# Two-layer recurrent kernel on one core: head of the next sequence one expert later on VectorE, last query product ahead of the second scores

## The reference, cut to what matters

```python
x = x + s * g
xn = _layernorm(x, axis=-1)
s = _L1_attn_ref(xn, ...)
g = _silu(_L1_ffn_ref(xn, ...))
x = x + s * g
```

## Time and profile before

| | |
|---|---|
| Median of 3 runs | 2175.03 us (2170.23 to 2177.49) |
| Profiled execution, its own time | 2173.18 us |
| Its span in the profile | 2171.3 us |
| Mean granted clock of TensorE | 0.971 of full speed |
| DVE | 1736.1 us busy, 80% |
| ACT | 978.4 us busy, 45% |
| POOL | 840.8 us busy, 39% |
| DMA | 151.20 MB, 70 GB/s on average |

### The profile page before, as it was taken

How to read it: one execution, slowest core, us unless ns; L and a number is a source line. 1 busy time by engine, 2 the same in 40 slices (tenths; PEclk the granted TensorE clock), 3 DMA queues, 4 the chain that set the end, 5 groups by cost and what they waited for, 6 DMA issues and landing times.

```text
span 2171.3 us, 37412 instructions
## 1 busy us (share of the span) xinstructions
PE 2023.1 (93%) x11786; PEld 1237.3 (57%) x11787; DVE 1736.1 (80%) x2890; ACT 978.4 (45%) x2532; POOL 840.8 (39%) x666
## 2 busy tenths in 40 slices
PE   7998599999889999999999999999999999999996
PEld 4554399998446545644564465456445544654563
DVE  5998466665398888889978988888898788888886
ACT  3544244443247236623833472275238235723841
POOL 1335300000353345346334633553463346336531
PEclk9999799999799999999999999999999999999998
DMA  6544521211412212212321122123022211211220
GB/s 180 154 136 147 166 59 51 58 51 51 134 46 65 58 49 60 62 37 54 81 72 39 50 64 54 49 66 81 16 68 65 69 39 54 59 54 49 73 56 10
DMA packets 145728, 151.20 MB, mean 70 GB/s; under 512 B 47664, under 2 KB 105648, under 8 KB 145584
## 3 DMA queue, kind: packets, MB, share of 16 engines
q1 hardware_dynamic: 138288, 136.73, 22.8%
q0 software_dynamic: 3072, 8.41, 1.2%
q10 hardware_dynamic: 4224, 4.19, 0.7%
HBM read 121.71 MB, written 27.43 MB: 69 GB/s over the span
## 4 chain that ended last, share of the span: by engine, by line
PE 35%; issue 16%; POOL 10%; DVE 9%; ACT 3%; DMA 1%; POOLq 0%; DVEq 0%; ACTq 0%
PE bank L1382 8%; PE bank L1241 6%; PE bank L1258 5%; PE bank L1295 3%; PE bank L1395 3%; POOL arena L2131 3%; PE bank L1268 2%; POOL arena L2143 2%; POOL arena L2146 2%; DVE arena L1842 2%; PE bank L1244 2%; PE bank L1174 2%; ACT arena L1623 2%; POOL arena L2123 2%; DMA arena<-gate_rows,arena 1%
## 5 line engine op out<-in xcount | busy, mean ns | idle before, releaser
L2123 POOL TENSOR_TENSOR arena<-arena 128x512 f32<-128x512 f32 x256 | 341.1, 1337 | 559.1 <-DVE arena L1842 545.2
L1382 PE MATMUL bank<-arena 128*128 128x256 f32 (+1 forms) x1120 | 384.4, 498 | 20.5 <-DVE arena L1987 20.5
L1842 DVE TENSOR_TENSOR_SCAN arena<-arena 128x512 f32<-128x512 f32 x256 | 356.1, 1391 | 1.1
L1174 PE MATMUL bank<-arena 128*128 128x512 f32 (+2 forms) x768 | 350.8, 603 | 1.0 <-ACT arena L1562 1.0
L1623 ACT ACTIVATE arena<-bank,arena 128x128 f32<-128x128 f32 (+3 forms) x512 | 266.3, 530 | 171.1 <-DVE arena L1822 171.1
L1382 PEld LDWEIGHTS bank<-arena 128*128 128x128 f32 x1120 | 214.4, 195 | 179.0 <-issue 131.0
L1822 DVE TENSOR_REDUCE arena<-bank 128x2 f32<-128x256 f32 (+3 forms) x256 | 208.4, 814 | 51.7 <-PE bank L1244 51.0
L1241 PE MATMUL bank<-arena 64*128 64x128 f32 (+3 forms) x1024 | 208.2, 483 | 41.0 <-ACT arena L1623 28.2
L1174 PEld LDWEIGHTS bank<-arena 128*128 128x128 f32 (+2 forms) x768 | 138.0, 187 | 185.0 <-issue 164.4
L1835 DVE TENSOR_TENSOR arena<-arena 128x512 f32<-128x512 f32 x256 | 220.7, 864 | 11.7 <-DMA arena<-values 10.1
L1632 ACT ACTIVATE arena<-bank 128x128 f32<-128x128 f32 (+3 forms) x512 | 196.5, 439 | 40.2 <-PE bank L1258 39.3
(11 more groups left out here) (207 smaller groups left out, 3032.4 us busy)
## 6 DMA issues: line engine op xcount, KB each, us to landing
arena<-values SPq DMA_DIRECT2D x256, 256.0 KB, 3.4
arena<-in_L_attn_h SPq DMA_DIRECT2D x16, 512.0 KB, 11.3
arena<-in_W1T SPq DMA_DIRECT2D x8, 1024.0 KB
arena<-in_W2T SPq DMA_DIRECT2D x8, 1024.0 KB
sorted_rows<-arena SPq DMA_DIRECT2D x42, 128.5 KB, 10.4
arena<-sorted_rows SPq DMA_DIRECT2D x40, 128.5 KB, 2.1
arena<-in_b2row SPq DMA_DIRECT2D x40, 128.0 KB, 2.9
gate_rows<-arena SPq DMA_DIRECT2D x39, 128.0 KB, 1.7
```

Of the source, the lines that this page charges most:

```text
L1174: last = nc.tensor.matmul(dst[rows, :], w, x, start=(n == 0), stop=(n == len(pairs) - 1))
L1382: last = nc.tensor.matmul(dst[o], w, x, start=first, stop=last_one)
L1842: nc.vector.tensor_tensor_scan(state[n % STATES][:, 1:T + 1], proj["w"][:, m, :], kv[n % 2], VEC["init"][:, m * HD + j:m * HD + j + 1], AL ...
L2123: nc.gpsimd.tensor_tensor(prods[(n + 2) % PRODS], state[n % STATES][:, 0:T], proj["r"][:, m, :], ALU.mult).then_inc(prod_done, 1)
```

## The change

Three edits, all in phase C:

- On DVE `head_gate` goes from between expert 1's sum and unit 26 to behind unit 27, after expert 2. `head_sum` goes from ahead of unit 27 to ahead of `head_stats`, after expert 3. `head_stats` stays.
- On PE `scores(1)` follows `query(7)`; it followed `query(6)`.
- On DVE `highest(1)` follows the rotation of q7; it followed that of q6.

The number of instructions is the same, and so are all semaphore values. Nothing changes on POOL, ACT and SP.

```diff
--- before.py
+++ after.py
@@ -1361,8 +1361,8 @@
                     i = int(name[-1]) if name != "lat" else 0
                     if name[0] == "q":
                         query(b, i)
-                        if name in ("q5", "q6"):
-                            scores(b, int(name[1]) - 5)
+                        if name in ("q5", "q7"):
+                            scores(b, (int(name[1]) - 5) // 2)
                     elif name == "lat":
                         pe.wait_ge(turned_q, 9 * b + 1)
                         begin(b, name, pre, pre_read)
@@ -1926,8 +1926,8 @@
                         nc.vector.tensor_tensor(bonus[:, m, :], bank[pre.bank(name)][:, :], proj["v"][:, m, :], ALU.mult).then_inc(v_read, 1)
                     if name[0] == "q":
                         rotate(m + 1)
-                        if name in ("q5", "q6"):
-                            highest(b, m - 5)
+                        if name in ("q5", "q7"):
+                            highest(b, (m - 5) // 2)
                 v.wait_ge(w_step, 2 * b + 2)
 
             def attention(b):
@@ -2028,15 +2028,13 @@
                 v.wait_ge(comb_done, 5 * b + 5)
 
                 def between(e):
-                    if not final:
-                        if e == 1:
-                            head_gate(b + 1)
-                        elif e == 2:
-                            head_sum(b + 1)
-                        elif e == 3:
-                            head_stats(b + 1)
+                    if not final and e == 3:
+                        head_sum(b + 1)
+                        head_stats(b + 1)
                     for n in EXPERT_UNITS.get(e, ()):
                         unit(b, n)
+                    if not final and e == 2:
+                        head_gate(b + 1)
                     if not final:
                         if e == 4:
                             head_shift(b + 1)
```

## The result

| | before | changed |
|---|---|---|
| Median | 2175.03 us (2170.23 to 2178.96, 5 runs) | 2155.42 us (2154.19 to 2158.79, 5 runs) |
| Profiled execution's span | 2171.3 us | 2152.3 us |
| DVE busy | 1736.1 us | 1754.9 us |
| Mean granted clock of TensorE | 0.971 | 0.972 |

The ratio is 0.9918, with a 95% interval of 0.9903 to 0.9933: the changed kernel is faster by 0.8%, 19.6 us between the medians. The forecast was 2156. DVE is busy for 18.8 us more than before with the same instructions, so some of them have become longer. This is where the 4.9 us of waiting per sequence went in part.

The account below looks back on a forecast made before the run. DVE, waiting for gathered gate rows, was taken to set the experts' pace. From 2173.2 us, less 17.1 (gate move) and 1.3 (sequence 2's excess), plus 1.6 (last query), came 2156 us; range 2141 to 2168.

Parts of the forecast that it names:

- What bounds the experts: Experts: DVE sets the pace; its gate waits 4.8 us per sequence for gathered rows, and PE then waits for `hidden`.
- The removed idle time, 4.9 us: Experts: moving the gate removes DVE's whole idle time, so `hidden` of expert 5 comes 4.9 us earlier per sequence.
- Rival 2: Experts: the wait for the gather comes back, leaving 1.0 us gained per sequence; 2166 us, chance 0.15.
- the distance from gate to gate: DVE, one sequence's gate to the next: falls from 196.65 to about 194.4 us if the forecast is right.
- What it gives back, 2.45 us: Experts: DVE's meetings with POOL cost 0.3 + 1.1 + 1.05 us, leaving 2.45 us gained per sequence.
- they take turns: Arena: DVE and POOL each wait for the end of the other's instruction; a meeting costs DVE 1.0 to 1.1 us.
- Rival 1: Experts: the turns with POOL cost nothing, as its products slip behind DVE's work; 2141 us, chance 0.22.
- The clock behind the gap: PE's matmuls after its gap run at a lower clock; DVE covers this except in sequence 2, worth 1.3 us.
- What is late next: Expert 7: PE's transposes wait about a microsecond for normalised rows, costing nothing more because DVE sets the end.
- Part 2, +1.6 us: Attention start: reordering the last query and highest(1) costs 0.2 us per sequence, 1.6 in all, bounds -4 to +10.
- One sign that was named as wrong: Attention start: ACT waits longer for L1822 and that stage's length grows; no size given.
- rival 4: Attention start: late exponentials and PE's lower clock (1.7 us) cost 3.0 us per sequence; 2179 us, chance 0.05.

Follow-up runs that it names:

- the short products: Changed kernel with POOL's products 25, 26 and 27 cut to 16 of 512 columns in every sequence; 2143.62 us, ratio 0.9862.
- the two other places of the gate: Changed kernel with the gate ahead of unit 27 (2152.56 us), or behind expert 3's sums next to the addition (2151.45 us).
- the query part alone: Kernel before, with only scores(1) put behind query(7) and highest(1) behind q7's rotation; 2177.17 us, ratio 1.0013.
- the gather early, on the changed kernel: Changed kernel with POOL's gather ahead of product 22 instead of between products 24 and 25; 2142.07 us, ratio 0.9852.

## Why the prediction was right

**What bounds the experts: right.** DVE's pace sets the stage. The gate's wait was the gap, and PE's gap followed from it. With all of the gap gone the stage would have been 50.0 us (the short products), which is 4.76 us less: 4.9 by the sum, 4.6 by PE's limit.

**The removed idle time, 4.9 us: right.** The new gate did not wait for the gather in any sequence. The margin was 0.8 us in the sum; with the gate one unit earlier a wait of 1.12 us came back. Rival 2 had the right mechanism, but not at this place. The forecast's own sign, the distance from gate to gate, fell from 196.65 us to 194.52 in two sequences (194.4 forecast) and lies at 194.9 to 195.8 in four more, whose attention was longer.

**What it gives back, 2.45 us: right in sum, wrong in its parts.** The third gather transfer's 0.3 us came as read from the earlier trace rows (1.26 for 0.95). Of the four terms then, the scan was to lose 0.3 us, the outer product 1.1 and the gate 1.05. Measured are 1.49, 0 and 0.88, in all 2.37. The step that failed is "they take turns", which I had read from the earlier trace rows: POOL started product 26 while the scan was already waiting for product 25, and went first again. Two products in a row then held the scan, and the outer product met none. Taking turns is not wrong everywhere, as the last section shows; it failed at scan 27. That the sum came out is partly luck: in either account there were a little over two meetings, of about a microsecond each. Rival 1, no cost, is refuted by the short products and by the two other places of the gate.

**The clock behind the gap: right, but its 1.3 us belong to one profile.** It was counted as nothing but in sequence 2, at 1.3 us. The stage of sequence 2 took 1.38 us more than its neighbour before (56.11 and 54.73), and 52.40 like all others after. But the run with the query part alone has the same gap, and there the clock stayed at its upper level behind it in six of seven sequences. This is its sequence 2, where the earlier trace rows have 8.45 us for the same 16 matmuls:

```profile
1133.04 5.43 PE L1382 MATMUL bank<-arena 128*128 128x256 f32 x16 [2.87 <-DVE arena L1987]
```

That stage took 54.77 us, no more than its neighbours. So DVE does cover the usual drop, and the excess was there in one of two profiles that have the gap: it is no steady part of what the move gives.

**What is late next: right.** PE waits 1.26 us in expert 7 (about a microsecond was forecast), and the end of the stage is DVE's.

**Part 2, +1.6 us: right in sign, too small by the wrong reasoning.** The readings of order came true: the exponentials of step 1 came 1.2 us later beside those of step 0 (1.3 forecast), the fourth scores 0.66 (0.7). I priced DVE's order, at +0.2 us per sequence. One sign that was named as wrong did appear here: ACT waits longer for L1822 (3.90 for 2.68 us), and the attention grew (753.4 for 752.1). Where the clock stays up, the new order is if anything 0.15 us shorter (93.11 and 93.26). What costs is the granted clock, which I had only in rival 4 and at 1.7 us per sequence. What a drop costs varies from 0.3 us to 1.5: in the changed kernel 93.51 in sequence 1 and 94.81 in sequence 6, where the lower clock lasts twice as long. Length is not all, for sequence 3 took 94.27 with a drop as short as that of sequence 1; what else decides stays open. Over the profiles it is 4.4 us for eight sequences (755.7 - 751.4, rounded), which lies in the bounds of -4 to +10; in the medians it is 0.4 to 3.1 us.

**The total.** 17.9 us from the experts for 17.1 + 1.3 = 18.4, 1.3 us back in the attention of that profile for 1.6: 16.6 us for 16.8. The profiled spans differ by 19.0, of which 2.5 us come from ahead of all edits, and the medians by 19.6, where the forecast started from 2173.2, 1.8 below the median. So the nearness of 2155.4 to 2156 owes something to chance.

## What to carry to other kernels

When an engine's wait is for a transfer that another engine issues, look at what that engine does meanwhile: moving the consumer back took away 4.8 us of waiting in each sequence and gave back half, while moving the issue into a gap of POOL's took it all away. A gap that is filled on the busy engine can be one in which a second engine worked undisturbed, so price each two-input instruction of DVE that now meets one of POOL, and let the number of products in arrears tell how many. And a wait of PE that holds up nothing may be better left alone: taking away the 1.36 us brought no time, and with it came other gaps, close together, and the lower clock in nearly every attention.

## What the runs showed that I had not expected

- DVE and POOL did not take turns at scan 27. Product 26 of POOL began while the scan had been waiting for 0.6 us, and the scan took 2.77 us, two products' worth. The Trainium skill, "SBUF — State Buffer", section "Who interferes with whom", says that a Vector instruction with two SBUF inputs contends with a GpSimd instruction that reads SBUF, and that the order of issue decides which of them blocks. With the recorded starts taken for the issue, the trace agrees for product 25 (1900.51, ahead of the scan's 1901.15) and not for product 26, which started 0.59 us after the scan and still went first.
- Elsewhere in the same trace they do take turns, also where POOL's products follow each other without a pause. In the attention of sequence 7, POOL first, then DVE:

```profile
1993.89 6.42 POOL L2121 TENSOR_TENSOR arena<-arena 128x512 f32<-128x512 f32 x4
...
1995.78 1.78 DVE L1842 TENSOR_TENSOR_SCAN arena<-arena 128x512 f32<-128x512 f32 x1
```

  The scan begins under the second of the four products and has waited 0.66 us when the third begins (1996.44); it takes 1.78 us, and the third product, 2.19 us long, waits for it. In the changed kernel's profile POOL goes twice only at scan 27, in all seven sequences. What decides it there stays open.
- The same gate behind the same product took 2.11 us in four sequences and 1.21 in three of one profile (the gather early, on the changed kernel), so this meeting is decided by little.
- Filling a gap of PE made the lower clock more frequent (46 of 48 attentions for 9 of 40), with PE's instructions unchanged. What lies between the two gaps and the drop was not isolated.
